# Windowed attention layers: the next sequence's input is transposed before the scores and copied before the exponentials

## The chip, the cores and the metric

The kernel runs on one core of a Trainium2 chip. The metric is the device time of one execution in microseconds; the median of three runs of the kernel before is 4236.15 us (4233.85 to 4240.07).

## The reference, cut to what matters

32 sequences of 128 tokens and 128 channels pass through a causal attention with 16 heads, a cross attention, and a feed-forward part that is itself six layers deep. Each of these six layers is a windowed attention followed by a gated MLP, and the change touches the windowed attention alone:

```python
def attn_layer(x, Wqkv, qs, ksc, Wo):          # x already had half its channels shifted by one token
    q, k, v = jnp.split(x @ Wqkv, 3, -1)       # 16 heads of 64, split with sh(...)
    q = l2norm(q) * qs
    k = l2norm(k) * ksc
    q = q * cos * scale + rotate_half(q) * sin * scale
    k = k * cos * inv + rotate_half(k) * sin * inv
    out = local_attention(q, k, v)             # each token sees the 32 before it
    return out @ Wo
```

## The kernel before, in words

All 32 sequences stay in SBUF in `y` for the six layers. In a windowed layer the work is cut into 128 steps: a step is one group of four heads of one sequence, so a sequence takes four steps and `j` counts eight steps, that is two sequences. The steps form a software pipeline: in step n the projections belong to head group n, and later parts belong to earlier groups (`WIN`, lines 61 to 70): head transposes to n-4, scores, maxima and exponentials to n-5, scaling to n-6, the turned probabilities and the value sums to n-7, the output projection to n-8. In this text "step 3" is a step with `j % 4 == 3` (j is 3 or 7), the last of a sequence, and "step 4" is the one right behind it (j is 4 or 0), "step 5" the next.

Each engine has its order written out by hand, and works it off in order:

- TensorE (`win_products`, L857, and `win_step`, L867): projection of queries and keys (L737, into bank 0), transposes of the probabilities (L797), projection of the values (L737, bank 7), transposes of the heads (L730, bank 3), output projection (L848, into the first 128 columns of bank 6), scores in two parts (L769 and L776, bank pairs 4/5 and 1/2), value sums (L828). Only in step 3, behind all of it, `win_turn_next` (L717) calls `win_input` (L707): two matmuls (L714 and L715; each shows as two in the trace) transpose the input of the sequence two ahead into columns 128 to 255 of bank 6. TensorE's program is written out for all steps; the others run as a loop of eight steps.
- VectorE (`win_step`, L1609): `by_cos` (L1550) and `by_sin` (L1558) from the projection, reciprocal and scaling of the probabilities (L1590, L1600), maxima of the scores (L1582), norms (L1565) and clamp (L1575). In step 1 it copies the next input (`tok`, L1526); in step 3 it takes the low part of the turned input (`xt_low`, L1532), which waits for ScalarE's copy, and then adds the finished output projection to `y` (L1607).
- ScalarE (`win_copies`, L1132, and `win_step`, L1139): copy of values and turned probabilities (L1120), squares (L1100), copy of the turned heads (L1091), four exponentials, each with an accumulator read (L1109), copy of the value sums (L1129). In step 3, behind all of it, `win_copy_next` (L1082) copies the turned input as its high part (`xt_high`, L1080).
- GpSimd (`win_step`, L1291): the rotated sum (L1269) in each step, the power of the norms (L1277) in each odd step, two multiplications by it (L1289) in each even step.
- SyncE's queue moves values within SBUF (L534), four transfers for two steps.

The first output projection of a sequence (L848 in step 4) overwrites bank 6, and so waits for VectorE's addition to `y` of step 3 and, like each L848, for the value sums that ScalarE copied in the step before:

```python
if jl % NG == 0:
    if has(b - 1):
        pe.wait_ge(c_yadd, layer * NB + b)
    pe.wait_ge(c_xsplit, layer * NB + xt_before(b))
pe.wait_ge(c_sum, m + 1)
```

The projection in step 5 may overwrite bank 0 once the squares of step 4 have been taken (L749), and the squares wait for `by_sin` (L1097). The value sums (L828) wait for VectorE's scaled probabilities of the same step (L817), which are behind `by_cos` and `by_sin` in VectorE's order. `win_step` is called for steps 5 to 127 of each layer; inputs two sequences ahead are turned in it 29 times in a layer, 174 times in all. The first inputs of a layer are turned elsewhere (L936, L959), and the five first steps call `win_products` and `win_copies`.

Of the kernel before, what the change touches and what calls it, by code (L numbers as in the profile page):

```python
# [140 lines left out]
def has(index):  # L141

    return not isinstance(index, int) or index >= 0
# [7 lines left out]
def build(nc, x_in, ctx_in, a_w, a_m, b_wq, b_bq, b_wk, b_bk, b_wv, b_bv, b_wo, b_bo, wqkv, q_scale, k_scale,  # L151
          wo, ln_g, ln_b, w1, b1, w2, b2, const_d, out):
    with ExitStack() as stack:
# [301 lines left out]
        def here(it, j, lag):  # L455
            return in_range(it, j, lag, (GROUPS, STEPS))
# [125 lines left out]
        def _(pe):  # L582
# [124 lines left out]
            def win_input(layer, b, slot):  # L707

                if not opening(b):

                    pe.wait_ge(c_xsplit, layer * NB + b)
                pe.wait_ge(c_tok, layer * NB + b + 1)
                dst = input_ps(b)
                nc.tensor.matmul(dst[0:DH, :], tok[slot][:, 0:DH], ident, start=True, stop=True)  # L714
                nc.tensor.matmul(dst[DH:P, :], tok[slot][:, DH:P], const("shift"), start=True, stop=True).then_inc(c_xturn, 1)  # L715

            def win_turn_next(layer, it, j):  # L717
                if j % NG == 3 and here(it, j, -2 * NG + 3):
                    win_input(layer, it * 2 + j // NG + 2, j // NG)
# [42 lines left out]
            def win_scores(layer, it, j, tiles):  # L762
                if here(it, j, WIN.scores):
                    jl = (j - WIN.scores) % STEPS
                    for lower, n, base in tiles:
                        for e in range(2):
                            rows, upper = slice(e * DH, (e + 1) * DH), lower // DH
                            at = e * DH + lower % DH
                            nc.tensor.matmul(win_ps[jl % 2][lower:lower + n, e, :].rearrange("q (i k) -> q i k", i=2),  # L769
                                             ident_b[rows, at:at + n], band_b[rows, upper, :].unsqueeze(1).to_broadcast([DH, 2, KEYS]),  # L770
                                             start=True, stop=False, skip_group_check=True, tile_position=(e * DH, lower))
                    for i in range(2):
                        for lower, n, base in tiles:
                            for e in range(2):
                                rows, q0, k0 = slice(e * DH, (e + 1) * DH), i * P + lower, (2 + i) * P + base
                                last = nc.tensor.matmul(win_ps[jl % 2][lower:lower + n, e, i * KEYS:(i + 1) * KEYS],  # L776
                                                        qk_t[jl % 4][rows, q0:q0 + n], qk_t[jl % 4][rows, k0:k0 + KEYS],
                                                        start=False, stop=False, skip_group_check=True, tile_position=(e * DH, lower))
                    last.then_inc(c_scores, 1)

            def win_upper_scores(layer, it, j):
                win_scores(layer, it, j, ((DH, PAD, BASES[1]), (DH + PAD, PAD, BASES[2])))
# [50 lines left out]
            def win_project_out(layer, it, j):  # L833
                if isinstance(it, int) and it == 0 and j == STEPS - 1:
                    pe.wait_ge(s_wo_in, 16 * (layer + 1))
                if here(it, j, WIN.out):
                    m = layer * GROUPS + it * STEPS + j - WIN.out
                    jl = (j - WIN.out) % STEPS
                    b = it * 2 + (j - WIN.out) // NG
# [6 lines that stand above are left out]
                    for i in range(2):  # L846
                        k = 2 * (jl % NG) + i
                        last = nc.tensor.matmul(acc_ps[:, 0:P], prob_t[(j - 1) % 2][:, i, :], wo_sb[:, k * P:(k + 1) * P],  # L848
                                                start=(k == 0), stop=(k == 2 * NG - 1))
                    if jl % NG == NG - 1:  # L850
                        last.then_inc(c_wo, 1)
# [2 lines left out]

                return min(NB, b + 4) if isinstance(b, int) else b + 4

            def win_products(layer, it, j):  # L857
                win_project(layer, it, j)
                win_turn_probs(layer, it, j)
                win_values(layer, it, j)  # L860
                win_heads(layer, it, j)
                win_project_out(layer, it, j)
                win_upper_scores(layer, it, j)
                win_lower_scores(layer, it, j)
                win_sum_values(layer, it, j)

            def win_step(layer, it, j):  # L867
                win_products(layer, it, j)
                win_turn_next(layer, it, j)

            def mlp_turn(layer, it, j):
                if here_q(it, j, 1):
# [127 lines left out]
        def _(act):  # L1000
# [81 lines left out]
            def win_copy_next(layer, it, j):  # L1082
                if j % NG == 3 and here(it, j, -2 * NG + 3):
                    win_input(layer, it * 2 + j // NG + 2, j // NG)

            def win_copy_heads(layer, it, j):
                if here(it, j, WIN.turn):
                    g = layer * GROUPS + it * STEPS + j - WIN.turn
                    jl = (j - WIN.turn) % STEPS
                    act.wait_ge(c_heads, g + 1)  # L1090
                    nc.scalar.activation(qk_t[jl % 4][:, :], heads_ps[:, :], ACT.Copy).then_inc(c_qk, 1)  # L1091

            def win_square(layer, it, j):
                if here(it, j, 0):
                    g = layer * GROUPS + it * STEPS + j

                    act.wait_ge(c_sin, g + 1)  # L1097
                    if has(it * STEPS + j - 1):
                        act.wait_ge(c_nrm2, g)
                    nc.scalar.activation(squares[:, :, :].rearrange("t h d -> t (h d)"), proj_ps[:, :], ACT.Square).then_inc(c_sq, 1)  # L1100

            def win_exponentials(layer, it, j):
                if here(it, j, WIN.exp):
                    m = layer * GROUPS + it * STEPS + j - WIN.exp
                    jl = (j - WIN.exp) % STEPS
                    act.wait_ge(c_top, m + 1)
                    for h in range(HG):
                        at = win_ps[jl % 2][:, h // 2, h % 2 * KEYS:(h % 2 + 1) * KEYS]
                        last = nc.scalar.activation(at, at, ACT.Exp, bias=top[jl % 2][:, h:h + 1], accum_out=psum_raw[jl % 2][:, h:h + 1])  # L1109
                    last.then_inc(c_exp, 1)  # L1110

            def win_copy_values(layer, it, j):
                fresh, turned = here(it, j, 0), here(it, j, WIN.probs)
                if fresh or turned:
                    if turned:
                        act.wait_ge(c_pturn, layer * GROUPS + it * STEPS + j - WIN.probs + 1)
                    if fresh:
                        act.wait_ge(c_vproj, layer * GROUPS + it * STEPS + j + 1)
                    cols = slice(0 if turned else 2 * P, 4 * P if fresh else 2 * P)
                    nc.scalar.activation(vout[j][:, cols], value_ps[:, cols], ACT.Copy).then_inc(c_vout, 1)  # L1120

            def win_copy_sums(layer, it, j):
                if here(it, j, WIN.value):
                    act.wait_ge(c_value, layer * GROUPS + it * STEPS + j - WIN.value + 1)
                    if last_sum(it, j):
                        for i in range(2):
                            last = nc.scalar.activation(prob_t[j % 2][:, i, :], last_sum_ps[i], ACT.Copy)
                    else:
                        last = nc.scalar.activation(prob_t[j % 2][:, 0:2, :], sum_ps[(j - WIN.scale) % 2], ACT.Copy)  # L1129
                    last.then_inc(c_sum, 1)  # L1130

            def win_copies(layer, it, j):  # L1132
                win_copy_values(layer, it, j)
                win_square(layer, it, j)
                win_copy_heads(layer, it, j)
                win_exponentials(layer, it, j)
                win_copy_sums(layer, it, j)

            def win_step(layer, it, j):  # L1139
                win_copies(layer, it, j)  # L1140
                win_copy_next(layer, it, j)

            def mlp_copy(layer, it, j):
                if here_q(it, j, 1):
# [699 lines left out]
```

## Time and profile before

| what | value |
|---|---|
| median of three runs | 4236.15 us (4233.85 to 4240.07) |
| the profiled execution | 4238.05 us, span 4236.2 us |
| PE busy | 3855.6 us, 91% |
| PEld (weight loads) | 3145.5 us, 74% |
| DVE busy | 3322.2 us, 78% |
| ACT busy | 3215.2 us, 76% |
| POOL busy | 3373.9 us, 80% |
| mean granted TensorE clock | 0.983 of full speed |

The span is counted from the first to the last instruction. PE is TensorE, PEld its weight loads, DVE is VectorE, ACT ScalarE, POOL GpSimd. Matmuls are pipelined and their ends are modelled, so their starts are the better marks. "<-" behind a row names what ended the idle time before it.

### The profile page before, as it was taken

To read this page: it belongs to the slowest core of one execution; us is meant where nothing else is said; L and a number is where in the kernel's file an instruction comes from. 1 tells how busy PE (TensorE), PEld (TensorE's weight loads), DVE (VectorE), ACT (ScalarE), POOL (GpSimd) and SP (SyncE) were. 2 spreads that over 40 slices of the span, in tenths; PEclk is the share of its full clock that TensorE was granted. 3 is DMA by queue.
4 is the path that set the end of the run, shared out by engine and by line. 5 is a ranking of instruction groups with operands and counts; after the bars stand their busy time and mean duration, and the time that the engine had idled before them with its cause. 6 is when DMAs were issued, how large, how long until landed. Compare 5 with 4: busy or idle time off the path is not lost.

```text
span 4236.2 us, 163553 instructions
## 1 busy us (share of the span) xinstructions
PE 3855.6 (91%) x61792; PEld 3145.5 (74%) x61792; DVE 3322.2 (78%) x8896; ACT 3215.2 (76%) x11601; POOL 3373.9 (80%) x2461
## 2 busy tenths in 40 slices
PE   7998886999989999889999899999899998999997
PEld 5665664877867777777777777777677777777786
DVE  7998887777777777777777687777777776877775
ACT  6988994888857888758888668887488886688884
POOL 4554447999968999869999689999599997899992
PEclk9999997999999999999999999999999999999999
DMA  3000001111112111111111121111111111111111
GB/s 83 0 0 1 0 0 31 35 37 35 36 37 52 36 36 35 38 52 35 36 35 35 35 55 35 36 36 37 51 37 35 37 35 36 39 35 35 37 35 43
DMA packets 302004, 145.50 MB, mean 34 GB/s; under 512 B 83989, under 2 KB 293779, under 8 KB 301459
## 3 DMA queue, kind: packets, MB, share of 16 engines
q1 hardware_dynamic: 301458, 137.25, 13.4%
q8 instruction: 461, 7.55, 0.8%
q14 instruction: 85, 0.69, 0.1%
HBM read 21.85 MB, written 2.10 MB: 6 GB/s over the span
## 4 chain that ended last, share of the span: by engine, by line
PE 56%; DVE 20%; ACT 11%; issue 10%; POOL 2%; DVEq 1%; SPq 0%; ACTq 0%; DMA 0%; POOLq 0%
PE bank L737 17%; PE bank L848 8%; PE pair L828 6%; PE pair L776 6%; PE bank L730 6%; ACT pair L1109 5%; PE pair L769 5%; PE pair L904 4%; DVE by_sin L1558 3%; PE bank L797 3%; DVE top L1506 3%; DVE top L1582 2%; DVE prob L1600 2%; DVE qk_parts L1481 2%; PE bank L920 1%
## 5 line engine op out<-in xcount | busy, mean ns | idle before, releaser
L1277 POOL TENSOR_TENSOR rnorm<-norm2g,neg_half 128x16 f32<-128x16 f32 x384 | 1115.5, 2905 | 147.1 <-DVE norm2g L1575 146.8
L1109 ACT ACTIVATE pair<-pair,top 128x64 f32<-128x64 f32 x3072 | 885.7, 290 | 265.0 <-DVE top L1582 265.0
L1269 POOL TENSOR_TENSOR rotated<-by_cos,by_sin 128x512 f32<-128x512 f32 x768 | 985.2, 1283 | 70.8 <-DVE by_sin L1558 68.8
L1289 POOL TENSOR_TENSOR rotated<-rotated,rnorm 128x512 f32<-128x512 f32 x768 | 784.9, 1043 | 0.5
L1100 ACT ACTIVATE squares<-bank 128x512 f32<-128x512 f32 x768 | 458.7, 597 | 355.9 <-DVE by_sin L1558 318.9
L737 PE MATMUL bank<-wqkv_high,xt_high 128*128 128x512 f32 (+1 forms) x1536 | 661.7, 431 | 12.7 <-ACT squares L1100 11.6
L1109 ACT ACTIVATION_READ_ACCUMULATOR pair<-pair,top 128x1 f32 x3072 | 638.7, 208 | 0.0
L776 PE MATMUL pair<-qk_t 64*32 64x64 f32 (+1 forms) x18432 | 608.9, 217 | 0.0
L1550 DVE TENSOR_TENSOR by_cos<-bank,rot_cos 128x512 f32<-128x512 f32 x768 | 528.2, 688 | 91.4 <-PE bank L737 64.4
L848 PE MATMUL bank<-wo_sb,prob_t 128*128 128x128 f32 x3072 | 531.4, 296 | 70.6 <-DVE y L1607 40.3
L828 PE MATMUL pair<-vout_all 64*64 64x64 f32 x6096 | 433.9, 227 | 118.3 <-DVE prob L1600 76.5
L1582 DVE TENSOR_REDUCE top<-pair 128x4 f32<-128x256 f32 x768 | 323.8, 422 | 265.8 <-PE pair L776 265.8
L848 PEld LDWEIGHTS bank<-wo_sb,prob_t 128*128 128x128 f32 x3072 | 405.0, 192 | 170.3 <-DVE y L1607 88.0
L1120 ACT ACTIVATE vout_all<-bank 128x512 f32<-128x512 f32 (+1 forms) x810 | 474.7, 586 | 73.0 <-PE bank L737 58.1
L1565 DVE TENSOR_REDUCE norm<-squares 128x8 f32<-128x512 f32 x768 | 519.0, 676 | 10.6 <-ACT squares L1100 10.0
L1558 DVE TENSOR_TENSOR by_sin<-bank,sin_now 128x512 f32<-128x512 f32 x768 | 521.9, 680 | 0.0
L737 PE MATMUL bank<-wqkv_low,xt_high 128*128 128x512 f32 (+1 forms) x1536 | 521.8, 340 | 0.0
L737 PE MATMUL bank<-wqkv_high,xt_low 128*128 128x512 f32 (+1 forms) x1536 | 521.6, 340 | 0.0
L1259 POOL TENSOR_TENSOR kz_parts<-qk_parts,cst 128x512 fp32r<-128x512 f32 x256 | 266.1, 1040 | 307.8 <-DVE qk_parts L1481 307.8
L730 PE MATMUL bank<-cst,rotated 128*128 128x128 f32 x3072 | 464.0, 274 | 0.0
L776 PEld LDWEIGHTS pair<-qk_t 64*32 64x32 f32 (+1 forms) x18432 | 458.3, 116 | 0.0
L1091 ACT ACTIVATE qk_t<-bank 128x512 f32<-128x512 f32 x768 | 455.2, 593 | 1.6 <-PE bank L730 1.6
(151 smaller groups left out, 9004.1 us busy)
## 6 DMA issues: line engine op xcount, KB each, us to landing
vmoved<-vout_all SPq DMA_DIRECT2D x1152, 64.0 KB, 2.1
ctx_all<-vout_all SPq DMA_DIRECT2D x384, 64.0 KB, 2.1
wqkv_sb<-in_L_ffn_Wqkv_dram SPq DMA_DIRECT2D x36, 256.0 KB, 3.9
ctx_all<-y SPq DMA_DIRECT2D x48, 128.0 KB
ctx_all<-y SPq DMA_DIRECT2D x48, 127.0 KB
wo_sb<-in_L_ffn_Wo_dram SPq DMA_DIRECT2D x6, 512.0 KB, 10.2
out_dram<-y SPq DMA_DIRECT2D x8, 256.0 KB, 3.5
w_sb<-in_L_ffn_W_dram SPq DMA_DIRECT2D x6, 341.0 KB, 3.3
```

The lines of the kernel that those rows point to most:

```text
L730: last = nc.tensor.transpose(heads_ps[:, k * P:(k + 1) * P], flat[:, k * P:(k + 1) * P], ident)
L737: last = nc.tensor.matmul(dst, a[slot][:, :], w[:, which, cols], start=(n == 0), stop=(n == 2))
L776: last = nc.tensor.matmul(win_ps[jl % 2][lower:lower + n, e, i * KEYS:(i + 1) * KEYS], qk_t[jl % 4][rows, q0:q0 + n], qk_t[jl % 4][rows, k ...
L828: last = nc.tensor.matmul(out_ps[e * DH:(e + 1) * DH, lower:lower + width], values_of(j, i, e, n), vout[j][rows, e * P + lower:e * P + low ...
L848: last = nc.tensor.matmul(acc_ps[:, 0:P], prob_t[(j - 1) % 2][:, i, :], wo_sb[:, k * P:(k + 1) * P], start=(k == 0), stop=(k == 2 * NG - 1))
L1109: last = nc.scalar.activation(at, at, ACT.Exp, bias=top[jl % 2][:, h:h + 1], accum_out=psum_raw[jl % 2][:, h:h + 1])
L1269: nc.gpsimd.tensor_tensor(rotated[j % 4][:, :, :, :], by_cos[j % 2][:, :, :, :], by_sin[j % 2][:, :, :, :], ALU.add).then_inc(c_rot, 1)
L1277: nc.gpsimd.tensor_tensor(rnorm[slot][:, :, :].rearrange("t g n -> t (g n)"), norm2g[slot][:, :, :].rearrange("t g n -> t (g n)"), neg_hal ...
L1289: nc.gpsimd.tensor_tensor(at, at, rnorm[slot][:, i, :].unsqueeze(2).to_broadcast([P, 2 * HG, DH]), ALU.mult).then_inc(c_unit, 1)
L1550: nc.vector.tensor_tensor(by_cos[j % 2][:, :, :, :], got, table(rot_cos, layer).unsqueeze(2).to_broadcast([P, 2, HG, DH]), ALU.mult).then_ ...
L1558: nc.vector.tensor_tensor(rows(by_sin[j % 2]), got, rows(sin_now), ALU.mult).then_inc(c_sin, 1)
L1565: nc.vector.tensor_reduce(pair[:, :, 0:1], squares[:, :, :], AX_X, ALU.add).then_inc(c_nrm2, 1)
```

## The change

TensorE's step is split in two: `win_whole_array` (projections, transposes, output projection) and `win_tiles` (scores and value sums). The turning of the next input now stands between the two. ScalarE's step is written out, and the copy of the turned input stands behind the copy of the heads, ahead of the exponentials. `win_products` and `win_copies` do what they did. VectorE, GpSimd and SyncE are as before.

```diff
@@ -854,19 +854,26 @@
-            def win_products(layer, it, j):
+            def win_whole_array(layer, it, j):
                 win_project(layer, it, j)
                 win_turn_probs(layer, it, j)
                 win_values(layer, it, j)
                 win_heads(layer, it, j)
                 win_project_out(layer, it, j)
+
+            def win_tiles(layer, it, j):
                 win_upper_scores(layer, it, j)
                 win_lower_scores(layer, it, j)
                 win_sum_values(layer, it, j)
 
+            def win_products(layer, it, j):
+                win_whole_array(layer, it, j)
+                win_tiles(layer, it, j)
+
             def win_step(layer, it, j):
-                win_products(layer, it, j)
+                win_whole_array(layer, it, j)
                 win_turn_next(layer, it, j)
+                win_tiles(layer, it, j)
 
@@ -1137,8 +1144,12 @@
             def win_step(layer, it, j):
-                win_copies(layer, it, j)
+                win_copy_values(layer, it, j)
+                win_square(layer, it, j)
+                win_copy_heads(layer, it, j)
                 win_copy_next(layer, it, j)
+                win_exponentials(layer, it, j)
+                win_copy_sums(layer, it, j)
```

## Rows read from the trace of the kernel before

**Rows 1.** Stretch, busy time (count) of PE, PEld, DVE, ACT, POOL; clock, DMA, GB/s:

```profile
1400.00:1700.00 300.00, 285.66 (x5391) 237.59 (x5390) 235.82 (x588) 242.22 (x925) 279.67 (x190) 1.00 0.15 36
```

**Rows 2.** The instructions of L1532 in 1400 to 1700 us:

```profile
L1532 DVE TENSOR_TENSOR xt_low<-bank,xt_high x19: 290/292/292, 1404.3 to 1689.4; 128x128 fp32r<-128x128 f32 x19
```

**Rows 3.** Waits of the whole span:

```profile
DVE xt_low L1532 <- ACT xt_high L1080: 179.9, 180, 1.7
PEld bank L848 <- DVE y L1607: 88.0, 174, 1.3
```

**Rows 4.** TensorE's timeline, from step 3 to the end of step 4:

```profile
1511.63 0.71 PE L848 MATMUL bank<-wo_sb,prob_t 128*128 128x128 f32 x4
...
1512.87 0.27 PE L828 MATMUL pair<-vout_all 64*64 64x64 f32 x1
...
1513.76 0.50 PE L737 MATMUL bank<-wqkv_high,xt_high 128*128 128x512 f32 x1
...
1515.98 0.71 PE L848 MATMUL bank<-wo_sb,prob_t 128*128 128x128 f32 x4 [0.23 <-DVE y L1607]
...
1517.75 0.27 PE L828 MATMUL pair<-vout_all 64*64 64x64 f32 x1 [0.26 <-DVE prob L1600]
...
1518.23 0.50 PE L737 MATMUL bank<-wqkv_high,xt_high 128*128 128x512 f32 x1
```

**Rows 5.** VectorE's timeline, around step 3 and step 4 (start, duration, line):

```profile
1506.95 0.17 DVE L1575 TENSOR_REDUCE norm2g<-norm 128x8 f32<-128x16 f32 x1
1507.18 0.29 DVE L1526 TENSOR_REDUCE tok<-y 128x128 f32 x1
...
1513.19 0.42 DVE L1582 TENSOR_REDUCE top<-pair 128x4 f32<-128x256 f32 x1 [0.55 <-PE pair L776]
...
1514.24 0.17 DVE L1575 TENSOR_REDUCE norm2g<-norm 128x8 f32<-128x16 f32 x1
1515.42 0.29 DVE L1532 TENSOR_TENSOR xt_low<-bank,xt_high 128x128 fp32r<-128x128 f32 x1 [1.01 <-ACT xt_high L1080]
1515.64 0.29 DVE L1607 TENSOR_TENSOR y<-y,bank 128x128 f32 x1
1515.86 0.69 DVE L1550 TENSOR_TENSOR by_cos<-bank,rot_cos 128x512 f32<-128x512 f32 x1
...
1517.27 0.42 DVE L1600 TENSOR_TENSOR prob<-pair,rsum 128x256 f32<-128x256 f32 x1
```

**Rows 6.** ScalarE's timeline in the same steps:

```profile
1513.65 0.29 ACT L1109 ACTIVATE pair<-pair,top 128x64 f32<-128x64 f32 x1 [0.44 <-DVE top L1582]
...
1514.82 0.39 ACT L1129 ACTIVATE prob_t<-pair 128x256 f32<-128x256 f32 x1
1515.09 0.30 ACT L1080 ACTIVATE xt_high<-bank 128x128 fp32r<-128x128 f32 x1
1515.35 0.60 ACT L1120 ACTIVATE vout_all<-bank 128x512 f32<-128x512 f32 x1
```

**Rows 7.** TensorE's weight loads (PEld): input transposes, and L848 in steps 5 and 6:

```profile
1513.39 0.13 PEld L714 LDWEIGHTS bank<-cst,tok 128*64 128x64 f32 x1
...
1519.95 0.53 PEld L848 LDWEIGHTS bank<-wo_sb,prob_t 128*128 128x128 f32 x4
...
1523.59 0.52 PEld L848 LDWEIGHTS bank<-wo_sb,prob_t 128*128 128x128 f32 x4
```

**Rows 8.** TensorE's waits in 1400 to 1700 us, the gap ahead of the projection:

```profile
PEld bank L737 <- issue: 3.3, 19, 0.2
```

**Rows 9.** GpSimd's timeline, from the first to the last of nine instructions back to back:

```profile
1507.20 2.91 POOL L1277 TENSOR_TENSOR rnorm<-norm2g,neg_half 128x16 f32<-128x16 f32 x1 [0.85 <-DVE norm2g L1575]
...
1513.34 1.27 POOL L1269 TENSOR_TENSOR rotated<-by_cos,by_sin 128x512 f32<-128x512 f32 x1
1514.58 2.89 POOL L1277 TENSOR_TENSOR rnorm<-norm2g,neg_half 128x16 f32<-128x16 f32 x1
...
1518.69 2.04 POOL L1289 TENSOR_TENSOR rotated<-rotated,rnorm 128x512 f32<-128x512 f32 x2
```

## The prediction

> **What bounds the kernel now.** I read the busy shares by stretch first, then the waits, then the timelines around one sequence boundary. In the steady part of a windowed layer TensorE is busy 95% and GpSimd 93% of the time [rows 1], so shares alone do not say what a shorter wait is worth. The period does: L1532 runs once in four steps, and 19 of them lie between 1404.3 and 1689.4 us [rows 2], so four steps take 285.1 / 18 = 15.84 us.
>
> The waits show what is odd at the sequence boundary. VectorE waits 179.9 us in 180 waits for ScalarE's `xt_high`, and TensorE's first output projection of a sequence waits for the addition to `y` 174 times [rows 3]. In the same boundary the value sums wait for the scaled probabilities [rows 4].
>
> The timelines tie them into one chain. In step 3 VectorE has clamped the norms by 1514.41 and then idles 1.01 us until `xt_high` is there [rows 5]. ScalarE takes that copy last, at 1515.09, behind four exponentials and the copy of the sums [rows 6], though the transposes it needs were issued by 1513.76 [rows 4, 7]. Only then come `xt_low`, the addition to `y` and `by_cos` of step 4, at 1515.42, 1515.64 and 1515.86 [rows 5]. So L848 of step 4 starts at 1515.98 with a wait for `y`, L828 at 1517.75 with a wait for `prob`, and the projection of step 5 at 1518.23 [rows 4]. Behind that the engines catch up and go at the plain pace: L848 to L848 takes 3.64 us (1519.95 to 1523.59) [rows 7], against 1515.98 - 1511.63 = 4.35 and 1519.95 - 1515.98 = 3.97 us around the boundary [rows 4, 7].
>
> **What the change removes.** With the copy ahead of the exponentials `xt_high` is done before VectorE comes to L1532. Its wait goes entirely. How close can L1532 follow the clamp? In step 1 `tok` follows it by 0.23 us, start to start (1506.95 to 1507.18) [rows 5]. Then L1532 would start at 1514.24 + 0.23 = 1514.47 in place of 1515.42: **0.95 us sooner**, and `y` and `by_cos` with it.
>
> **What it adds.** The transposes cost TensorE the same time, but now ahead of the scores. In step 3 the next projection starts 1513.76 - 1512.87 = 0.89 us behind the first value sum; in step 4, without inputs, 1518.23 - 1517.75 = 0.48 [rows 4]. So they cost c = 0.41 us, of which 0.17 (3.3 us in 19) is a gap ahead of the projection that no wait explains [rows 8]. In the new place c is not shown. Bounds: 0.24 if that gap does not come back, 0.58 if such a gap is paid twice, once on either side. I take 0.41, since the old place too lies between two shapes of the array: the transposes load 128*64 tiles [rows 7] between 64*64 and 128*128 [rows 4], and in the new place stand between 128*128 and the small tiles of the scores. The Trainium skill ("TensorEngine Tiling (Array Packing)", Key Properties) says that a change of the tiling mode, not of the tile, drains TensorE. By that rule both orders make one change more than a step without inputs, so it gives no saving and speaks against the hope that grouping whole-array work is worth something by itself; the sum would stay as it is.
>
> Everything that follows the scores of step 3 comes c later. The maxima start at 1513.60 instead of 1513.19; VectorE only idles longer ahead of them (0.55 us now) [rows 5]. Norms and clamp follow in VectorE's order, so what counts is 0.95 - c = 0.54 us: `xt_low` at 1514.88, `y` at 1515.10, `by_cos` at 1515.32.
>
> On ScalarE the copy is moved past eight instructions of the exponentials and the copy of the sums. It takes 0.27 us there (1514.82 to 1515.09 is the spacing of its neighbour) and falls into the idle time ahead of the exponentials, 0.44 us now [rows 6] and 0.85 with c. It waits for the transposes, and the exponentials are queued behind that wait; but they need the maxima of scores that TensorE issues behind the transposes, so the new wait cannot end last. I cost it at nothing; if the cover were gone, it would be 0.27 us in the chain to L848. No DMA belongs to a moved step. GpSimd's queue and SyncE's are passed by nothing; SyncE's transfers wait for the copy of the values, which in step 4 follows the copy of the sums directly: 1514.82 + 0.41 + 0.27 = 1515.50, against 1515.35 [rows 6], and is wanted by value sums at 1517.2 only.
>
> **What is late next.** L848 of step 4 needs `y` (now 1515.10 + 0.29 = 1515.39) and the sums: their copy starts at 1515.23, and L848 started 1515.98 - 1514.82 = 1.16 behind it only for `y` [rows 4, 6]. The copy lasts 0.39, and L848 starts 0.05 behind what it waits for (1515.64 + 0.29 to 1515.98) [rows 4, 5], so at about 1515.23 + 0.39 + 0.05 = 1515.67: 0.31 us sooner. The scaled probabilities come 0.54 sooner, so L828 at 1517.21, and the scores issued from 1515.67 are through 1.24 us behind (1512.87 - 1511.63, step 3 [rows 4]), at 1516.91. The probabilities still come last, by 0.30. The projection of step 5 then starts at 1518.23 - 0.54 = 1517.69. Steps 5, 6 and 7 keep their pace of 3.64 us, so the 0.54 us stays won: a period of 15.30 us.
>
> Is GpSimd quick enough? Nine instructions from 1507.20 to 1520.73 run back to back: two L1277, three L1269, four L1289 [rows 9]. Four steps have one L1269 more, about 1.24 us (1513.34 to 1514.58), so the floor is 13.53 + 1.24 = 14.77 us, 0.53 under the new period. It has room.
>
> **The sum.** 174 boundaries x 0.54 = 94 us. The layers' ends, the MLPs and the first two attentions stay. Against the profiled execution, 4238.05 - 94 = 4144; that execution is 1.9 us over the median, so the median would be **4142 us**.
>
> **The rivals.**
> 1. The transposes are cheap behind whole-array work, c = 0.24: 0.95 - 0.24 = 0.71 us x 174 = 124 us, 4113 us. For it: the unexplained 0.17 us [rows 8]. Against: the array still changes shape. Chance 0.17.
> 2. The chain of the exponentials takes over: scores, maxima, exponentials, sums, L848. If the new period is set by it at the boundary, only L848's 0.31 us is won: 54 us, 4182 us. For it: plain steps go at 3.64 us by just this chain. Against: the probabilities are 0.30 us later than it in step 4. Chance 0.10.
> 3. GpSimd becomes the bound, should c be small and the rest pull together: (15.84 - 14.77) x 174 = 186 us at most, 4050 us; it would cap a larger gain, not undo this one. Chance 0.05.
> 4. Slower: c stands in the chain ahead of the maxima, where before it stood beside it. The gain is 0.95 - c, so from c = 0.95 on the kernel loses. With the drain on both sides costing as much as a whole output projection each (0.71 us by its row [rows 4]) c would be 0.24 + 1.42 = 1.66 and the loss 0.71 x 174 = 124 us, 4360 us. Nothing in the trace shows such a gap; from L848 at 1511.63 to the value sums at 1512.87 the array changes shape already [rows 4]. Chance 0.05.
> 5. Nothing: another wait of the same size stands behind the one removed, the way the stall of `xt_low` hid one for the projection. `by_cos` of step 4 needs its projection, which started at 1513.76 and would be ready by about 1514.8 [rows 4], under the new 1515.32. Chance 0.03.
>
> My forecast has the rest, 0.60.
>
> **The range.** The bounds of c alone give 4112 to 4172. Down to 4098 it also takes in part of rival 3, up to 4186 rival 2; about 0.15 stays outside. A change of 0.2%, some 8 us, is about what a measurement of this kernel can tell from none. Faster by more: forecast, rivals 1, 2 and 3, 0.92; within 0.2%: 0.03; slower: 0.05.
>
> **What would show it.** In the profile of the changed kernel the wait of `xt_low` for `xt_high` is gone; the copy `xt_high` stands between `qk_t` and the first exponential; the maxima of step 3 start 1.56 + c behind L848 (now 1.56) [rows 4, 5], which measures c; L848 of step 4 waits for `prob_t` of ScalarE, not for `y`; L828 of step 4 still waits for `prob`; the period is 15.3 us and GpSimd is busy 97% of it. The forecast is wrong if the wait of L1532 stays, if the maxima come more than 0.6 us later, or if the period is under 15.1 or over 15.5 us.

## The result and the profile after

The changed kernel takes **4128.84 us** (median of four runs, 4125.96 to 4130.01), against 4236.5 us before (4233.85 to 4240.07 in the same comparison): a ratio of 0.9744, 95% interval 0.9727 to 0.9761. The forecast was 4142 us with a range of 4098 to 4186. The gain is 107.7 us, where 94 were forecast.

In the page's table of busy time the engines do what they did before, in a shorter span:

```profile
span 4124.1 us, 163553 instructions
PE 3836.9 (93%) x61792; PEld 3140.8 (76%) x61792; DVE 3319.2 (80%) x8896; ACT 3198.5 (78%) x11601; POOL 3373.8 (82%) x2461
```

The busy times of VectorE and GpSimd are within 3 us of before, those of TensorE and ScalarE 19 and 17 us lower. So the 112.1 us that the span lost (4236.2 - 4124.1) were for the most part idle time. The waits in 1400 to 1700 us say whose; these rows answer to [rows 3] and [rows 8] (engine, line, whom it waited for: us in total, times, longest):

```profile
DVE top L1593 <- PE pair L776: 35.2, 69, 0.9
ACT pair L1116 <- DVE top L1593: 23.5, 59, 0.6
...
PEld pair L828 <- DVE prob L1611: 4.7, 10, 0.5
PEld bank L848 <- issue: 3.8, 20, 0.2
PE pair L828 <- DVE prob L1611: 3.3, 10, 0.3
PEld pair L769 <- issue: 3.3, 19, 0.2
DVE by_cos L1561 <- issue: 3.2, 10, 0.3
DVE by_cos L1561 <- POOL rotated L1280: 3.2, 10, 0.3
```

In this stretch no wait of `xt_low` for `xt_high` is left, and none of L848 for `y` (over the whole span 6 of either are left, out of 180 and 174 waits). The value sums wait for the probabilities 10 times, not at each of the 19 boundaries. L848's 20 waits are put down to "issue", not to ScalarE's copy of the sums, as the prediction had it; the starts fit the copy, which ends at 1521.48 + 0.39 = 1521.87, while L848 of step 4 loads its weights from 1521.99. VectorE's timeline around one boundary answers to [rows 5]:

```profile
1519.85 0.42 DVE L1593 TENSOR_REDUCE top<-pair 128x4 f32<-128x256 f32 x1 [0.92 <-PE pair L776]
1520.19 0.68 DVE L1576 TENSOR_REDUCE norm<-squares 128x8 f32<-128x512 f32 x1
1520.90 0.17 DVE L1586 TENSOR_REDUCE norm2g<-norm 128x8 f32<-128x16 f32 x1
1521.00 0.29 DVE L1543 TENSOR_TENSOR xt_low<-bank,xt_high 128x128 fp32r<-128x128 f32 x1
1521.24 0.29 DVE L1618 TENSOR_TENSOR y<-y,bank 128x128 f32 x1
1521.46 0.69 DVE L1561 TENSOR_TENSOR by_cos<-bank,rot_cos 128x512 f32<-128x512 f32 x1
...
1522.87 0.42 DVE L1611 TENSOR_TENSOR prob<-pair,rsum 128x256 f32<-128x256 f32 x1
```

From the maxima to `by_cos` it takes 1521.46 - 1519.85 = 1.61 us; before it was 1515.86 - 1513.19 = 2.67. ScalarE's timeline one boundary earlier answers to [rows 6]: the copy stands ahead of the exponentials, which still wait 0.63 us behind it.

```profile
1503.53 0.59 ACT L1098 ACTIVATE qk_t<-bank 128x512 f32<-128x512 f32 x1
1504.01 0.28 ACT L1087 ACTIVATE xt_high<-bank 128x128 fp32r<-128x128 f32 x1
1504.92 0.29 ACT L1116 ACTIVATE pair<-pair,top 128x64 f32<-128x64 f32 x1 [0.63 <-DVE top L1593]
```

TensorE's timeline, in steps 3 and 4 of the boundary that the VectorE rows show, answers to [rows 4]:

```profile
1517.92 0.71 PE L848 MATMUL bank<-wo_sb,prob_t 128*128 128x128 f32 x4
1518.56 0.32 PE L714 MATMUL bank<-cst,tok 128*64 128x128 f32 x1
...
1520.05 0.50 PE L737 MATMUL bank<-wqkv_high,xt_high 128*128 128x512 f32 x1
...
1522.02 0.68 PE L848 MATMUL bank<-wo_sb,prob_t 128*128 128x128 f32 x4
...
1523.35 0.27 PE L828 MATMUL pair<-vout_all 64*64 64x64 f32 x1
...
1523.83 0.50 PE L737 MATMUL bank<-wqkv_high,xt_high 128*128 128x512 f32 x1
```

The maxima start 1519.85 - 1517.92 = 1.93 us behind L848; before it was 1.56. So **c = 0.37 us**, where c is what the transposes add ahead of the scores. And from L848 of step 3 to the next projection TensorE takes 1520.05 - 1517.92 = 2.13 us, before 1513.76 - 1511.63 = 2.13 [rows 4]: placing the transposes next to the other whole-array work saved TensorE nothing. The same measure gives the price of the transposes in their old place. In step 2, without them, the trace of before has 1509.75 - 1507.98 = 1.77 us, so they cost 2.13 - 1.77 = 0.36 there:

```profile
1507.98 0.71 PE L848 MATMUL bank<-wo_sb,prob_t 128*128 128x128 f32 x4
...
1509.75 0.50 PE L737 MATMUL bank<-wqkv_high,xt_high 128*128 128x512 f32 x1
```

The measure that the rest of this text uses is the period, the time from one `xt_low` to the next in VectorE's timeline. It alternates, since VectorE's, ScalarE's and GpSimd's programs are loops of eight steps, two boundaries each: one boundary lies within the body, the other where the loops turn round. The turn shows as 0.33 us of "issue" ahead of `by_cos`. The periods are read between 1400 and 1700 us. Before, the two are 15.60 and 16.08 us (15.84 on average); after, 14.98 and 15.38 (15.18 on average, forecast 15.30). The medians and ratios come from five comparisons, each with its own runs of the kernel before, whose medians lie between 4235.2 and 4236.9 us:

| kernel | median us | ratio (95% interval) | period within the body | at the turn |
|---|---|---|---|---|
| before | 4236.5 | | 15.60 | 16.08 |
| the change | 4128.84 | 0.9744 (0.9727 to 0.9761) | 14.98 | 15.38 |
| pe_only | 4311.15 | 1.0175 (1.0158 to 1.0192) | 15.97 | 16.45 |
| act_only | 4107.38 | 0.9694 (0.9678 to 0.9710) | 15.02 | 15.02 |
| twice | 4169.9 | 0.9847 (0.9831 to 0.9863) | 15.20 | 15.60 |
| sums_first | 4079.39 | 0.9632 (0.9616 to 0.9648) | 14.73 | 15.23 |
| early_split | 4101.55 | 0.9682 (0.9666 to 0.9698) | 15.00 | 15.03 |
| early_both | 4039.11 | 0.9535 (0.9519 to 0.9551) | 14.44 | 14.87 |
| half_pow | 4127.46 | 0.9745 (0.9728 to 0.9761) | 14.99 | 15.38 |
| sums_half_pow | 4079.12 | 0.9628 (0.9612 to 0.9644) | 14.74 | 15.23 |
| early_both_half | 4029.76 | 0.9514 (0.9498 to 0.9530) | 14.44 | 14.87 |
| old_sums | 4035.55 | 0.9532 (0.9516 to 0.9548) | 14.43 | 14.85 |
| two_parts | 4034.06 | 0.9520 (0.9504 to 0.9535) | 14.68 | 14.68 |
| two_parts_half | 3885.05 | 0.9166 (0.9150 to 0.9181) | 13.66 | 14.15 |

### The profile page after: what moved, and what is told of

The parts are those of the page before. It is cut to its first block, busy times and chain, and to the rows that moved or that the text cites. A ratio compares the mean times of both kernels' runs of the same rounds, so it can differ in the third digit from the quotient of the medians.

```text
span 4124.1 us, 163553 instructions
## 1 busy us (share of the span) xinstructions
PE 3836.9 (93%) x61792; PEld 3140.8 (76%) x61792; DVE 3319.2 (80%) x8896; ACT 3198.5 (78%) x11601; POOL 3373.8 (82%) x2461
## 3 DMA queue, kind: packets, MB, share of 16 engines
q1 hardware_dynamic: 301458, 137.25, 13.7%
## 4 chain that ended last, share of the span: by engine, by line
PE 68%; DVE 17%; issue 7%; ACT 5%; POOL 2%; DVEq 1%; SPq 0%; DMA 0%; ACTq 0%; POOLq 0%
PE bank L737 20%; PE bank L848 10%; PE pair L776 7%; PE bank L730 7%; PE pair L828 6%; PE pair L769 6%; PE pair L911 4%; PE bank L797 4%; DVE top L1517 3%; DVE qk_parts L1492 2%; PE bank L714 2%; PE bank L927 2%; DVE by_sin L1569 1%; DVE by_sin L1485 1%; DVE ctx_all L1678 1%
## 5 line engine op out<-in xcount | busy, mean ns | idle before, releaser
L1288 POOL TENSOR_TENSOR rnorm<-norm2g,neg_half 128x16 f32<-128x16 f32 x384 | 1116.3, 2907 | 64.6 <-DVE norm2g L1586 64.2
L848 PE MATMUL bank<-wo_sb,prob_t 128*128 128x128 f32 x3072 | 536.3, 298 | 30.7 <-ACT prob_t L1136 27.7
L848 PEld LDWEIGHTS bank<-wo_sb,prob_t 128*128 128x128 f32 x3072 | 404.7, 192 | 129.6 <-issue 39.5
L828 PE MATMUL pair<-vout_all 64*64 64x64 f32 x6096 | 434.1, 227 | 63.2 <-issue 40.3
```

What stands on the lines that cost most here:

```text
L828: last = nc.tensor.matmul(out_ps[e * DH:(e + 1) * DH, lower:lower + width], values_of(j, i, e, n), vout[j][rows, e * P + lower:e * P + low ...
L1288: nc.gpsimd.tensor_tensor(rnorm[slot][:, :, :].rearrange("t g n -> t (g n)"), norm2g[slot][:, :, :].rearrange("t g n -> t (g n)"), neg_hal ...
```

## The experiments

### The two halves of the change

**pe_only** keeps TensorE's new order and puts ScalarE's back:

```diff
             def win_step(layer, it, j):
-                win_copy_values(layer, it, j)
-                win_square(layer, it, j)
-                win_copy_heads(layer, it, j)
+                win_copies(layer, it, j)
                 win_copy_next(layer, it, j)
-                win_exponentials(layer, it, j)
-                win_copy_sums(layer, it, j)
```

> Only TensorE's half of the change: the transposes stand ahead of the scores, ScalarE still copies the turned input last. Theory A (the gain is the end of VectorE's wait for xt_high; the transposes cost c = 0.36 us in the chain ahead of the maxima): scores, exponentials, xt_high, xt_low and by_cos all come 0.36 us later, a period of 15.84 + 0.36 = 16.20 us and about 4236 + 174 x 0.36 = 4299 us, with the wait of xt_low still some 1 us. Theory B (keeping whole-array work together saves TensorE time by itself): 4236 us or less.

Measured: 4311.15 us, slower than before by 75 us. VectorE's timeline in step 3, with the full wait still in it:

```profile
1500.10 0.42 DVE L1589 TENSOR_REDUCE top<-pair 128x4 f32<-128x256 f32 x1 [0.92 <-PE pair L776]
...
1501.15 0.17 DVE L1582 TENSOR_REDUCE norm2g<-norm 128x8 f32<-128x16 f32 x1
1502.33 0.29 DVE L1539 TENSOR_TENSOR xt_low<-bank,xt_high 128x128 fp32r<-128x128 f32 x1 [1.01 <-ACT xt_high L1087]
```

VectorE idles 0.92 us ahead of the maxima (0.55 before) and then its 1.01 us all the same. Both periods grow by 0.37 us: the price c, paid with nothing bought. Over 174 boundaries that is 64 us. Theory B falls: TensorE's half by itself costs time.

Another part is TensorE's clock. In this profile, which is the longest of the four executions (4317.75 us), eight periods take 18.0 us in place of 16.4, some 12.5 us in all. In each of them the mean granted clock is 0.90 or 0.91, in the normal ones next to two of them 1.00. One of them, TensorE's timeline and the busy time from 2250.70 to 2253.90 us (the third number from the end is the granted clock):

```profile
2247.94 0.71 PE L848 MATMUL bank<-wo_sb,prob_t 128*128 128x128 f32 x4 [0.61 <-DVE y L1614]
...
2250.19 0.27 PE L828 MATMUL pair<-vout_all 64*64 64x64 f32 x1 [0.74 <-DVE prob L1607]
...
2250.70 0.79 PE L737 MATMUL bank<-wqkv_high,xt_high 128*128 128x512 f32 x1
```

```profile
2250.70:2253.90 3.20, 3.20 (x16) 2.80 (x13) 1.92 (x6) 1.91 (x10) 2.24 (x3) 0.50 0.00 0
```

TensorE had waited 0.61 and 0.74 us in the step before, then the clock stood at its lower level for 3.2 us, and the projection took 0.79 us in place of 0.50. The same two waits stand at other turns of the loop without it (at 1518.87 and 1521.12 us, with a clock of 1.00 from 1405 to 1700 us), so they do not decide it alone. The shortest of the four executions (4305.65 us) is 12.1 us under the profiled one, as if it had none of these periods, but it has no profile. It is 69 us over before, so some 5 us beside the 64 stay unexplained.

**act_only** keeps ScalarE's new order and puts TensorE's back:

```diff
             def win_step(layer, it, j):
-                win_whole_array(layer, it, j)
+                win_products(layer, it, j)
                 win_turn_next(layer, it, j)
-                win_tiles(layer, it, j)
```

> Only ScalarE's half: the copy of the turned input stands ahead of the exponentials, TensorE transposes behind the value sums as before. Theory A: the copy now waits for the end of the transposes, so the exponentials start about 0.5 us later than before the change, against 0.36 us in the full change, but VectorE's wait for xt_high is gone and by_cos is up to 1.1 us sooner. The chain of the exponentials then sets both kinds of boundary, 3 x 3.64 + 4.15 = 15.07 us, where the full change has 14.98 and 15.38: about 4110 us, 0 to 35 us under the full change's 4129. Theory B: without the grouping on TensorE most of the gain is gone, 4180 us or more.

Measured: 4107.38 us, 21 us **under** the full change. The maxima of step 3 and ScalarE's timeline show the new wait, for the transposes at the end of TensorE's step:

```profile
1514.92 0.59 ACT L1097 ACTIVATE qk_t<-bank 128x512 f32<-128x512 f32 x1
1515.48 0.42 DVE L1592 TENSOR_REDUCE top<-pair 128x4 f32<-128x256 f32 x1 [0.54 <-PE pair L776]
1516.17 0.28 ACT L1086 ACTIVATE xt_high<-bank 128x128 fp32r<-128x128 f32 x1 [0.66 <-PE bank L715]
1516.35 0.28 ACT L1115 ACTIVATE pair<-pair,top 128x64 f32<-128x64 f32 x1
```

The exponentials are held up by the copy, though their maxima were through at 1515.90 (1515.48 + 0.42); yet the kernel is faster than the full change, since c no longer stands ahead of the maxima. Both periods are 15.02 us, near the 15.07 expected if one chain, that of the exponentials, sets both boundaries. The full change has nearly the same period within the body (14.98) and 0.36 us more at the turn (15.38), where VectorE's chain carries the turn of the loop as well. ScalarE's half by itself gains 129 us, the two halves together 108.

### The price of the transposes in their new place

**twice** issues each input's transposes a second time, onto the same columns, in the steps' loop:

```diff
-                nc.tensor.matmul(dst[0:DH, :], tok[slot][:, 0:DH], ident, start=True, stop=True)
-                nc.tensor.matmul(dst[DH:P, :], tok[slot][:, DH:P], const("shift"), start=True, stop=True).then_inc(c_xturn, 1)
+                for n in range(1 if opening(b) else 2):
+                    nc.tensor.matmul(dst[0:DH, :], tok[slot][:, 0:DH], ident, start=True, stop=True)
+                    last = nc.tensor.matmul(dst[DH:P, :], tok[slot][:, DH:P], const("shift"), start=True, stop=True)
+                last.then_inc(c_xturn, 1)
```

> The full change, with the two transposes of an input issued twice over in the steps' loop (the second time onto the same columns). Theory A: they stand in the chain ahead of the maxima in each boundary, so the maxima of step 3 come another 0.24 to 0.36 us later and the kernel takes 42 to 63 us more, 4171 to 4192 us. Theory C (TensorE's 0.15 us of slack in a step, or VectorE, covers them): 4129 to 4140 us.

Measured: 4169.9 us, 41 us more than the change, both periods longer by 0.22 us. The second pair costs 41 / 174 = 0.24 us a boundary, 0.22 by the periods, so TensorE's time ahead of the scores lies on the path. c is 0.37, so there are 0.15 us that the second pair does not pay. In size they fit the gap of 0.17 us that stood ahead of the projection before and now stands ahead of L769 (3.3 us in 19, in both traces). That this gap is the change of shape is likely, and not shown apart.

### What sets the pace after the change

**sums_first** copies the value sums ahead of the exponentials:

```diff
                 win_copy_next(layer, it, j)
-                win_exponentials(layer, it, j)
                 win_copy_sums(layer, it, j)
+                win_exponentials(layer, it, j)
```

> The full change, and ScalarE copies the value sums ahead of the exponentials of the same step, so that L848 of the next step no longer waits for the exponentials. Theory A (at boundaries inside a body of eight steps, and in all plain steps, that chain sets the pace at 3.64 us a step): plain steps go at TensorE's own 3.49 us until GpSimd's floor of 14.77 us for four steps binds; boundaries of 14.8 to 15.0 us, 4060 to 4100 us. Theory D (VectorE or GpSimd sets the pace already, or the exponentials, now later, hold up the scaled probabilities): 4120 us or more.

Measured: 4079.39 us, 49 us under the change. Both periods fall, by 0.25 within the body and by 0.15 at the turn. The chain scores - maxima - exponentials - sums - L848 had held the period within the body.

**half_pow** and **sums_half_pow** make GpSimd's work lighter, on the change and on sums_first: they leave out the power of the second head group's norms and use the first group's for both. The rows show L1288 at 1644 ns in place of 2.9 us:

```diff
-                    nc.gpsimd.tensor_tensor(rnorm[slot][:, :, :].rearrange("t g n -> t (g n)"), norm2g[slot][:, :, :].rearrange("t g n -> t (g n)"),
-                                            neg_half[:, :], ALU.pow).then_inc(c_rn, 1)
+                    nc.gpsimd.tensor_tensor(rnorm[slot][:, 0, :], norm2g[slot][:, 0, :],
+                                            neg_half[:, 0:2 * HG], ALU.pow).then_inc(c_rn, 1)
...
-                        nc.gpsimd.tensor_tensor(at, at, rnorm[slot][:, i, :].unsqueeze(2).to_broadcast([P, 2 * HG, DH]), ALU.mult).then_inc(c_unit, 1)
+                        nc.gpsimd.tensor_tensor(at, at, rnorm[slot][:, 0, :].unsqueeze(2).to_broadcast([P, 2 * HG, DH]), ALU.mult).then_inc(c_unit, 1)
```

> The full change, with GpSimd's power of the norms taken of the first of two head groups only, and used for both: the second group's norms are left out, GpSimd's 2.9 us instruction becomes shorter. Theory A (GpSimd is 97% busy and still not what sets the pace): 14.98 and 15.38 us as before, 4120 to 4135 us. Theory F (GpSimd sets it, at least at one boundary in two, where by_cos is shown waiting 0.33 us for its rotated sum): 4100 us or less.

> sums_first, with the power of the first of two head groups only, as in half_pow: the second group's norms are left out. Theory A: in sums_first GpSimd's floor sets the 14.73 us boundary, so that one shrinks to TensorE's own time, 4 x 3.49 + 0.37 = 14.3 us, and the other one, VectorE's 15.23 us, stays: about 4079 - 87 x 0.4 = 4044 us. Theory G (14.73 us is TensorE or the exponentials again): 4070 us or more.

Measured: 4127.46 and 4079.12 us, the same as without it. The first is as theory A has it. The second is a miss. I had taken the 14.73 us of sums_first for GpSimd's floor, since my own sum had put that at 14.77. With 2.5 us of GpSimd's work gone the period stays 14.74. VectorE's timeline of sums_half_pow, step 3 and 4, shows the real holder:

```profile
1505.87 0.42 DVE L1593 TENSOR_REDUCE top<-pair 128x4 f32<-128x256 f32 x1 [0.81 <-PE pair L776]
...
1507.03 0.29 DVE L1543 TENSOR_TENSOR xt_low<-bank,xt_high 128x128 fp32r<-128x128 f32 x1
1507.27 0.29 DVE L1618 TENSOR_TENSOR y<-y,bank 128x128 f32 x1
1507.49 0.69 DVE L1561 TENSOR_TENSOR by_cos<-bank,rot_cos 128x512 f32<-128x512 f32 x1
```

VectorE waits for the scores and then works without a gap until `prob`, for which TensorE waits (L828 for `prob`: 9.0 us in 20). So it is VectorE's chain at both boundaries, and the two differ by 0.49 us, about the turn of the loop. That a period equals an engine's floor proves nothing until that engine's work is made shorter.

**early_split** takes `xt_low` and the addition to `y` out of that chain, into VectorE's idle time ahead of the maxima. ScalarE copies the turned input ahead of the heads (first VectorE's step, then ScalarE's):

```diff
                 win_scale(layer, it, j)
+                win_split_next(layer, it, j)
+                win_add(layer, it, j)
                 win_max(layer, it, j)
                 win_norms(layer, it, j)
                 win_clamp(layer, it, j)
                 win_tok_next(layer, it, j)
-                win_split_next(layer, it, j)
-                win_add(layer, it, j)
...
                 win_square(layer, it, j)
-                win_copy_heads(layer, it, j)
                 win_copy_next(layer, it, j)
+                win_copy_heads(layer, it, j)
                 win_exponentials(layer, it, j)
```

> The full change, with ScalarE's copy of the turned input ahead of the copy of the heads, and VectorE's xt_low and addition to y ahead of the maxima, in its idle 0.9 us. Theory A (at the boundary where the eight-step loops turn round, VectorE's chain maxima - norms - clamp - xt_low - y - by_cos - prob sets the 15.38 us; at the other boundary the chain of the exponentials sets 14.98): the first loses some 0.4 us, the second nothing, 15.0 us for both, about 4129 - 87 x 0.40 = 4094 us. Theory E (GpSimd or the turn of the loop itself sets the 15.38): 4120 us or more.

Measured: 4101.55 us; the period at the turn falls from 15.38 to 15.03, the other stays (15.00). As theory A has it, a little short of the 4094 us expected: in the timeline `xt_low` waits for ScalarE's copy, and the maxima start directly behind `y`, with no idle time left ahead of them.

```profile
1513.16 0.29 DVE L1543 TENSOR_TENSOR xt_low<-bank,xt_high 128x128 fp32r<-128x128 f32 x1 [0.42 <-ACT xt_high L1087]
1513.39 0.29 DVE L1618 TENSOR_TENSOR y<-y,bank 128x128 f32 x1
1513.65 0.42 DVE L1593 TENSOR_REDUCE top<-pair 128x4 f32<-128x256 f32 x1
```

**early_both** adds the order of sums_first to early_split (`win_copy_sums` ahead of `win_exponentials`).

> As early_split, and the copy of the sums ahead of the exponentials too. Theory A: both chains are out of the way and GpSimd's floor sets both boundaries, 14.7 to 14.8 us: about 4079 - 87 x 0.45 = 4040 us. Theory E (the turn of the loop sets one boundary in two): 4070 us or more.

Measured: 4039.11 us, 14.44 and 14.87 us. Against the change, either repair alone gains 27 or 49 us, both together 90: each chain hid part of what the other's repair was worth.

### The floor under all of it

GpSimd shows 300.00 us busy in 300 in early_both. **early_both_half** is early_both with the edit of half_pow.

> early_both, with the power of the norms of the first of two head groups only, used for both: the second group's norms are left out, which takes 2 x 1.25 us from GpSimd's four steps. Theory A (in early_both GpSimd is busy 300.00 of 300 us and sets the pace, 14.65 us on average): the period falls to TensorE's own 4 x 3.49 + 0.37 = 14.3 us, by 0.3 us and more, to 3980 us or thereabouts. Theory G (the engines' hand-overs set it, GpSimd only fills up, as in sums_half_pow): 4030 us or more.

Measured: 4029.76 us, both periods unchanged (14.44 and 14.87). The 9 us between the medians are not in the steady part: the periods of all six layers add up to only 1.9 us less. The four executions of early_both lie between 4033.82 and 4042.17 us, and the two long ones have a mean granted clock of 0.979, the others 0.983 and 0.984. So GpSimd at 100% did not set the period by itself here, and theory A falls a second time.

**old_sums** has TensorE's and VectorE's order of before the change, and a new order on ScalarE alone: heads, value sums, turned input, exponentials. Against the change its ScalarE part is:

```diff
                 win_copy_heads(layer, it, j)
+                win_copy_sums(layer, it, j)
                 win_copy_next(layer, it, j)
                 win_exponentials(layer, it, j)
-                win_copy_sums(layer, it, j)
```

> TensorE's order as before the change; ScalarE copies the heads, the value sums, then the turned input, then takes the exponentials. Theory A: the transposes are out of VectorE's chain again (c = 0), so its chain gives 16.08 - 1.09 = 14.99 us where the loops turn and 14.5 us at the other boundary, and L848 does not wait for the exponentials: 14.75 us on average, about 4236 - 174 x 1.08 = 4048 us, 30 us under sums_first. Theory B (the grouping on TensorE helps by itself) or theory H (the exponentials, behind the end of TensorE's step, hold up the scaled probabilities): as sums_first, 4079 us, or more.

Measured: 4035.55 us, as early_both, with the same periods of 14.43 and 14.85. Two different orders end at one figure, with TensorE busy 298 of 300 us in each. ScalarE's timeline in step 3 (the sums wait for TensorE, the copy for nothing, the exponentials for nothing):

```profile
1509.15 0.38 ACT L1135 ACTIVATE prob_t<-pair 128x256 f32<-128x256 f32 x1 [0.22 <-PE pair L828]
1509.48 0.28 ACT L1086 ACTIVATE xt_high<-bank 128x128 fp32r<-128x128 f32 x1
1509.65 0.29 ACT L1115 ACTIVATE pair<-pair,top 128x64 f32<-128x64 f32 x1
```

**two_parts** is old_sums without the third partial product of each projection (low part of the input, high part of the weights), 0.36 us less for TensorE in a step. **two_parts_half** also has the edit of half_pow.

```diff
-                parts = ((xt_high, wqkv_high), (xt_high, wqkv_low), (xt_low, wqkv_high))
+                parts = ((xt_high, wqkv_high), (xt_high, wqkv_low))
                 for n, (a, w) in enumerate(parts):
-                    last = nc.tensor.matmul(dst, a[slot][:, :], w[:, which, cols], start=(n == 0), stop=(n == 2))
+                    last = nc.tensor.matmul(dst, a[slot][:, :], w[:, which, cols], start=(n == 0), stop=(n == 1))
```

> old_sums with the third of the three partial products of each projection (low part of the input with high part of the weights) left out: TensorE has 0.36 us less to do in each step. Theory I (TensorE alone sets the pace of old_sums, 14.43 and 14.85 us; GpSimd, also at 300.00 of 300 us, has room yet): the period falls by 0.5 us or more, below 14.2 us, and the kernel to under 3960 us. Theory J (GpSimd is at its floor as well): 14.5 us or more, 4010 us or more.

> two_parts, with the power of the norms of the first of two head groups only (the second group's norms left out as well), 2 x 1.25 us less for GpSimd in four steps. Theory I: the same as two_parts within 20 us. Theory J: here both are relieved, and only here the period falls, to 13.0 to 14.0 us, VectorE's chain permitting, 60 us or more under two_parts.

Measured: 4034.06 and 3885.05 us. Against old_sums a lighter TensorE alone gains 1.5 us, and with GpSimd lighter too 150 us; a lighter GpSimd alone was tried on early_both only, and left its periods as they were. In two_parts both periods are 14.68 us, TensorE waits for GpSimd (first row; 0.2 us in one wait in old_sums), and GpSimd has no gap. Here is its floor:

```profile
PEld bank L730 <- POOL rotated L1299: 20.3, 40, 0.9
```

```profile
1400.00:1700.00 300.00, 283.12 (x5651) 233.53 (x5649) 255.93 (x633) 262.37 (x1004) 300.00 (x206) 1.00 0.16 38
```

(Columns of the second: stretch, busy time and count of PE, PEld, DVE, ACT and POOL, clock, DMA share, GB/s.) The mean period of old_sums is (14.43 + 14.85) / 2 = 14.64, so TensorE and GpSimd reach their floors within 0.04 us of each other. Theory J holds: GpSimd's 300 of 300 us did mean that it had no room, and it could not be seen while TensorE stood at its own floor. early_both and old_sums end there, and a further gain would need less work on both.

## Why the prediction was right, and by how much it missed

- **The wait that goes.** Right. VectorE's 1.01 us ahead of `xt_low` and L848's wait for `y` are gone.
- **How close `xt_low` follows the clamp.** Mis-sized: I took 0.23 us from `tok`; it is 0.10 (1520.90 to 1521.00). The part of VectorE's chain that is won is 1.08 us, not 0.95. From the maxima to `by_cos` 2.67 - 1.61 = 1.06 us are won, the same within 0.02.
- **The price c.** Close: 0.41 forecast, 0.37 measured, with the bounds 0.24 and 0.58. The 0.41 was read from the first value sum to the projection, and that start is not alike in the two steps: in step 3 it lies among the last scores, in step 4 behind all of them. Read from L848 it would have been 0.36. That its new place lies in the chain ahead of the maxima is what pe_only and twice show. The rule of the Trainium skill ("TensorEngine Tiling (Array Packing)", Key Properties), that a change of tiling mode drains TensorE, agrees with the gap of 0.17 us that moved with the transposes, and with 2.13 us in both orders; no run here separates the drain from other causes of the gap.
- **The gain of a boundary.** By these two sizes VectorE's chain would win 1.06 - 0.37 = 0.69 us, not 0.54. At the turn it did: 16.08 - 15.38 = 0.70. Within the body 15.60 - 14.98 = 0.62 were won. There the step "What is late next" fell short: it let the probabilities come last by 0.30 us, and that margin was used up. VectorE came 0.15 us sooner than forecast. L848 of step 4 came 4.10 us behind that of step 3 where 4.04 was forecast, and from there to the first value sum it took 1.33 us where 1.24 was forecast, a figure read from a step 3. L828 of step 4 shows no wait within the body, and sums_first shows that the chain of the exponentials, rival 2, held this boundary.
- **Rival 2's price.** Wrong: if that chain took over, 0.31 us were to be won, 4182 us. It took over at every second boundary, and 0.62 us were won there all the same. The price counted only the way from L848 to L848 across step 3 (4.35 us, now 4.10), and not the next one, which the prediction itself had at 3.97 against the plain 3.64 [rows 4, 7]: it is plain now too.
- **The sum.** 174 x (0.62 + 0.70) / 2 = 115 us, beside 112.1 of the span and 107.7 of the medians; the forecast of 94 was 13.7 us too careful. That the error stayed small is in part luck: the gain of VectorE's chain was put 0.15 us too low, and that a second chain would hold half of the boundaries, which costs 0.08 us at each of those, was left out.
- **ScalarE's copy costs nothing.** Right: 0.28 us in idle time, and 0.63 us of that idle time remain behind it.
- **GpSimd has room.** Right for this change (half_pow; GpSimd is busy 292.39 of 300 us, 97% as forecast), and its floor of 14.77 us was 14.68 in two_parts.
- **Slower from c = 0.95 on.** Not reached; pe_only shows the mechanism: with nothing won on VectorE, c is a pure loss.
- **What the prediction did not ask** is whether both halves are needed. They are not: act_only beats the change by 21 us. The prediction says that the moved copy waits for the transposes, and takes their earlier place as given. It did not weigh that an earlier transposition is paid in two chains, VectorE's and that of the exponentials, while a later copy is paid only in that of the exponentials.

## What to carry to other kernels

Where two engines are reordered together, run each half alone: here one half by itself gained 129 us, and the other took 21 us of it away. Ask of a moved instruction which chains it now stands in, not only which wait it ends. When a chain goes in a loop over several engines, the next one can lie close behind it (here 0.04 us between the floors of TensorE and GpSimd), so repairs must be tried in pairs. Whether an engine sets the pace by itself is shown by making its work shorter, not by its busy share; and where that brings nothing, a second engine at its floor may hide it.

## What the runs showed that was not expected

- A GpSimd that is busy 300.00 of 300 us need not be the only one to set the pace: with 2.5 us in 14.65 of its work taken away the periods of early_both stayed (early_both_half), and only with TensorE lighter as well did they fall (two_parts_half).
- GpSimd's rows get longer as it fills up: in 1400 to 1700 us L1277's kind takes 2906 ns before, 2955 ns in old_sums and 2987 ns in two_parts on average. That need not be slower work, since the rows overlap: those of old_sums add up to 121.2 + 108.5 + 87.1 = 316.8 us in a stretch of 300.
- The power of 128x16 elements takes GpSimd 2.91 us, that of 128x8 takes 1.64 us. From these two I estimate 0.16 us a column and 0.4 us besides.
- A name behind "<-" can be a coincidence. In the changed kernel `by_cos` of step 5 behind the turn is shown waiting 0.33 us for GpSimd's rotated sum, 3.2 us in 10; in half_pow, with GpSimd lighter, the same wait of 3.1 us in 10 is put down to TensorE's projection, and the time is the same.
